# Attention in rounds of four steps in place of two, with one exponential instruction for both heads

## What is computed

```
x = x + _L0_attn_a_ref(_layernorm(x), ...)   # state space: scan over tokens, gelu, norm
x = x + _L0_ffn_ref(_layernorm(x), ...)      # channel mixer with token shift
x = x + _L0_attn_b_ref(_layernorm(x), ...)   # causal attention, 16 heads of 64
x = x + _L0_ffn_ref(_layernorm(x), ...)      # the same mixer again
```

```
latent_kv = x @ w_kv_down                     # 256 -> 128
kv = latent_kv @ w_kv_up; k, v = ...          # 16 heads of 64 each
q = (x @ w_q).reshape(Bx, Tx, N_HEAD, HEAD_SIZE)
att = jnp.einsum('bqhd,bkhd->bhqk', q, k) * scale
att = jnp.where(causal, att, -jnp.inf)
att = jax.nn.softmax(att, axis=-1)
y = jnp.einsum('bhqk,bkhd->bqhd', att, v).reshape(Bx, Tx, HD)
return y @ w_out
```

## Time and profile before

| | |
|---|---|
| median of 3 runs | 2115.67 us (2113.73 to 2116.21) |
| profiled execution, first to last instruction | 2113.7 us |
| its own time | not given apart from the span |
| mean granted TensorE clock | 0.980 |
| TensorE busy | 1984.7 us, 94% |
| VectorE busy | 1337.2 us, 63% |
| ACT busy | 1097.9 us, 52% |
| GpSimd busy | 1425.9 us, 67% |

### The profile page before, as it was taken

The page is one execution under the profiler, slowest core; times in us unless marked ns, Lnnn a source line. Parts: engine busy times, 40 slices in busy tenths (PEclk is TensorE's granted clock), DMA queues, the critical chain, the costliest instruction groups (busy, mean ns, idle before and its releaser), DMA issues.

```text
span 2113.7 us, 35206 instructions
## 1 busy us (share of the span) xinstructions
PE 1984.7 (94%) x12886; PEld 1240.9 (59%) x12886; DVE 1337.2 (63%) x2728; ACT 1097.9 (52%) x2236; POOL 1425.9 (67%) x812
## 2 busy tenths in 40 slices
PE   8997788999999999999989999999999999999898
PEld 6775454555655555555555655555555555555466
DVE  7786555576656666666665657576756575656443
ACT  5775543455545454545455444545445445444585
POOL 1333225778687878787857687868786878687822
PEclk9998899999999999999999999999999999999999
DMA  3000000000000000000000000000000000000001
GB/s 124 1 1 1 0 7 13 13 19 10 13 18 16 13 19 12 19 10 19 13 12 17 12 20 11 17 12 20 11 18 11 20 11 18 11 14 11 26 26 60
DMA packets 29243, 37.01 MB, mean 18 GB/s; under 512 B 6928, under 2 KB 20368, under 8 KB 29072
## 3 DMA queue, kind: packets, MB, share of 16 engines
q1 hardware_dynamic: 29072, 34.76, 5.4%
HBM read 30.02 MB, written 4.46 MB: 16 GB/s over the span
## 4 chain that ended last, share of the span: by engine, by line
PE 63%; DVE 14%; POOL 12%; ACT 6%; issue 4%; DMA 1%; POOLq 0%; ACTq 0%; SPq 0%; DVEq 0%
PE heads_out L918 16%; POOL acc L1416 10%; PE beside L723 9%; PE scores L723 7%; PE two_heads L874 7%; PE scores L897 4%; PE scores L903 4%; PE scores L899 4%; PE scores L901 4%; DVE part_max L1112 3%; ACT prob L1331 2%; PE two_heads L723 2%; PE beside L929 2%; PE heads_out L723 1%; DVE wQK_lo L1073 1%
## 5 line engine op out<-in xcount | busy, mean ns | idle before, releaser
L1416 POOL TENSOR_TENSOR acc<-acc,prob 128x1024 f32<-128x1024 f32 (+3 forms) x512 | 1017.9, 1988 | 195.4 <-ACT prob L1331 140.1
L1331 ACT ACTIVATE prob<-scores 128x512 f32<-128x512 f32 (+3 forms) x1280 | 579.4, 539 | 649.2 <-PE scores L903 289.0
L1112 DVE TENSOR_REDUCE part_max<-two_heads 128x2 f32<-128x1024 f32 x384 | 469.3, 1222 | 280.5 <-PE two_heads L874 279.7
L918 PE MATMUL heads_out<-prob,V 128*64 128x512 f32 (+3 forms) x2560 | 544.4, 547 | 0.0
L1109 DVE CUSTOM_DVE_ANT_0 two_heads<-two_heads,mask 128x128 f32<-128x128 f32 (+3 forms) x512 | 242.0, 514 | 180.4 <-PE two_heads L874 180.4
L874 PE MATMUL two_heads<-k_hi,q_hi 64*128 64x512 f32 (+3 forms) x1280 | 274.1, 424 | 62.8 <-DVE part_max L1112 30.6
L918 PEld LDWEIGHTS heads_out<-prob,V 128*64 128x64 f32 x2560 | 156.7, 137 | 232.4 <-issue 209.6
L874 PEld LDWEIGHTS two_heads<-k_hi,q_hi 64*128 64x128 f32 x1280 | 120.6, 184 | 256.6 <-issue 133.4
L897 PE MATMUL scores<-q_hi,k_hi 64*128 64x512 f32 (+3 forms) x1280 | 236.1, 364 | 0.8 <-DVE k_lo L1100 0.5
L903 PE MATMUL scores<-neg_max,sel 64*128 64x512 f32 (+3 forms) x1280 | 235.6, 362 | 0.0
L901 PE MATMUL scores<-q_lo,k_hi 64*128 64x512 f32 (+3 forms) x1280 | 235.5, 362 | 0.0
(11 more groups left out here) (301 smaller groups left out, 2898.7 us busy)
## 6 DMA issues: line engine op xcount, KB each, us to landing
rden<-rden_rows SPq DMA_DIRECT2D x128, 128.0 KB, 2.9
X<-u SPq DMA_DIRECT2D x8, 512.0 KB, 8.7
out<-X SPq DMA_DIRECT2D x8, 512.0 KB, 2.9
wQK_raw<-wQuery SPq DMA_DIRECT2D x16, 192.0 KB, 3.1
wO_raw<-wOut SPq DMA_DIRECT2D x16, 128.0 KB, 2.8
wV_raw<-wValue SPq DMA_DIRECT2D x8, 128.0 KB, 2.9
den<-den_rows SPq DMA_DIRECT2D x64, 4.0 KB
rden_rows<-den SPq DMA_DIRECT2D x64, 4.0 KB, 1.3
```

The source lines that it names most:

```text
L918: made = pe.matmul(heads_out[head(h), x0:], V[vn % NVS][:, tt, p % 2, head(h)], prob[step % NPROB][:, h, x0:], start=t == 0, stop=t == TPB ...
L1112: made = ve.reduce_max(part_max[:, t, :, c:c + 1], two_heads[:, :, 0:width], AX.X)
L1331: ac.activation(prob[step % NPROB][:, h, x0:], bank(task, h)[:, x0:], ACT.Exp).then_inc(empty(task, h)[0], 1)
L1416: po.tensor_tensor(total[:, :, x0:], total[:, :, x0:], new[:, :, x0:], ALU.add).then_inc(acc_ok, 1)
```

## The change

A round has four steps. Its order is: a maximum, two score tasks, a maximum, the due `invert`, two more score tasks, the rest of the maxima (the first of them in banks 5 and 6, the next in banks 0 and 1, a third in banks 2 and 3), then the four `weigh` and `accumulate` of the same round with `two_parts` after the second of them, `scale_out`, then up to four side tasks in banks 7, 3, 2 and 1 (`SIDE`); `denominators` takes the place of the first, and the fourth runs only if it is due within 8 steps. The products with V are no longer one round behind. `maximum` takes the pair of banks that the plan names (`pair_of`). A score task has both its banks as one entry, with one semaphore step for both heads, and ACT's exponential is one instruction over both heads. Due times at a unit's end and those of the last mixer's first tasks move by some steps.

```diff
 NG = 3
+SIDE = [7, 3, 2, 1]
 DVE_OUT = 62
...
-        self.side_bank = 7
+        self.side_bank, self.max_bank = 7, 5
...
         elif kind == "maximum":
-            self.take(task, (5, 6))
+            self.take(task, (self.max_bank, self.max_bank + 1))
         elif kind == "score":
             n = 2 * (self.step_of[task[1:]] % 2)
             if task[2] >= TPB * UNITS[task[1]][2]:
                 self.masked[task[1:]] = len(self.masked) + 1
-            self.take(task, (n,), (n + 1,))
+            self.take(task, (n, n + 1))
...
-        ahead = {-14: [("channel_start", "b"), ("mixer_weights", "b"), ("turn_normal", "b", 0)],
-                 -12: [("turn", "b", 0), ("turn_normal", "b", 1)], -10: [("turn", "b", 1), ("mix_tokens", "b", 0)],
-                 -4: [("turn_normal", "b", 2)], 0: [("mix_tokens", "b", 1)]}
+        ahead = {-16: [("channel_start", "b"), ("mixer_weights", "b"), ("turn_normal", "b", 0)],
+                 -12: [("turn", "b", 0), ("turn_normal", "b", 1)], -8: [("turn", "b", 1), ("mix_tokens", "b", 0)],
+                 -4: [("turn_normal", "b", 2), ("mix_tokens", "b", 1)]}
...
-            later.extend([(s + 2, ("denominators", idx)), (s + 6, ("invert", idx)), (s + 8, ("scale_out", idx)), (s + 10, ("two_parts", idx))])
+            later.extend([(s + 4, ("denominators", idx)), (s + 8, ("invert", idx)), (s + 8, ("scale_out", idx)), (s + 12, ("two_parts", idx))])
...
-        for s in range(0, len(steps) + 2, 2):
+        for s in range(0, len(steps), 4):
             self.in_steps = True
-            if s == 2:
-                self.heads_free = self.freed[4]
             for load in sorted(x for x in loads if x[0] <= s and self.layers_done):
                 loads.remove(load)
                 self.need(*load[1])
             for b in [STATS_BEFORE[UNITS[i]] for i in range(NU) if s == self.start[i] and UNITS[i] in STATS_BEFORE]:
                 side += self.mixer_stats(b, 2 if b else 3, NT)
             urgent = max([self.start[i] + TPB * (UNITS[i][2] + 1) for i in range(NU) if self.start[i] <= s + 4])
-            goal = min(len(self.maxima), max(urgent, min(s + 2 + LEAD, self.at + 3))) if self.layers_done else urgent
+            goal = min(len(self.maxima), max(urgent, min(s + 4 + LEAD, self.at + 5))) if self.layers_done else urgent
             if self.at < goal:
                 maximum()
-            due("invert")
             for step in steps[s:s + 2]:
                 self.need("score", *step)
+            if not s:
+                self.in_steps = False
+                yield
+                self.in_steps = True
             if self.at < goal:
                 maximum()
             else:
                 chore()
-            filler(10 ** 6)
-            diagonal = not steps[s:s + 2] or any(t >= TPB * UNITS[idx][2] for idx, t in steps[s:s + 2])
-            if not diagonal:
-                self.side_bank = 0
-                filler(s + 8)
-                self.side_bank = 7
-            while self.at < goal - 1:
+            due("invert")
+            for step in steps[s + 2:s + 4]:
+                self.need("score", *step)
+            self.max_bank = 5
+            while self.at < goal:
                 maximum()
-            for idx, t in steps[max(0, s - 2):s]:
+                self.max_bank = (5, 0, 2)[(5, 0, 2).index(self.max_bank) - 2]
+            self.max_bank = 5
+            if not s:
+                self.heads_free = self.freed[4]
+            for idx, t in steps[s:s + 4]:
                 self.need("weigh", idx, t)
                 self.need("accumulate", idx, t)
+                if (idx, t) == steps[s + 1]:
+                    due("two_parts")
                 if t == TPB * (UNITS[idx][2] + 1) - 1:
                     self.need("take_out", idx)
                     output(idx)
-            if self.at < goal:
-                maximum()
-            due("two_parts")
             due("scale_out")
-            if not due("denominators") and diagonal:
-                filler(s + 8)
+            for n, self.side_bank in enumerate(SIDE):
+                if n or not due("denominators"):
+                    filler(10 ** 6 if n < 3 else s + 8)
+            self.side_bank = 7
             if side:
-                self.add_all(side.pop(0))
+                for piece in (side.pop(0), side.pop(0) if side else []):
+                    self.add_all(piece)
             self.add_all(ahead.get(s - len(steps), []))
             self.in_steps = False
             yield
+        s = len(steps)
...
+        def pair_of(task):
+            first = plan.bank[task][0][0][0]
+            return two_heads if first == 5 else scores[:, first:first + 2, :]
...
-                        made = pe.matmul(two_heads[:, h, 0:width], q[head(h), t * P:(t + 1) * P], k[head(h), 0:width], start=True, stop=True)
+                        made = pe.matmul(pair_of(task)[:, h, 0:width], q[head(h), t * P:(t + 1) * P], k[head(h), 0:width], start=True, stop=True)
...
-                    for h in range(2):
-                        for s, v in free(task, h):
-                            w.wait_ge(s, v)
+                    for s, v in free(task):
+                        w.wait_ge(s, v)
+                    first = plan.bank[task][0][0][0]
                     w.wait_ge(*empty(("query", idx)))
                     w.wait_ge(*empty(("turn_max", idx)))
                     w.wait_ge(*empty(("key", idx - j + c)))
                     w.wait_ge(att_const, 4)
                     for h in range(2):
-                        pe.matmul(bank(task, h)[:, x0:], k_hi[g][head(h), kc], q_hi[i][head(h), x0:], start=True, stop=False)
+                        pe.matmul(scores[:, first + h, x0:], k_hi[g][head(h), kc], q_hi[i][head(h), x0:], start=True, stop=False)
                     for h in range(2):
-                        pe.matmul(bank(task, h)[:, x0:], k_lo[g][head(h), kc], q_hi[i][head(h), x0:], start=False, stop=False)
+                        pe.matmul(scores[:, first + h, x0:], k_lo[g][head(h), kc], q_hi[i][head(h), x0:], start=False, stop=False)
                     for h in range(2):
-                        pe.matmul(bank(task, h)[:, x0:], k_hi[g][head(h), kc], q_lo[i][head(h), x0:], start=False, stop=False)
+                        pe.matmul(scores[:, first + h, x0:], k_hi[g][head(h), kc], q_lo[i][head(h), x0:], start=False, stop=False)
                     for h in range(2):
-                        pe.matmul(bank(task, h)[:, x0:], sel[head(h), :], neg_max[idx % NMAX][head(h), x0:], start=False, stop=True).then_inc(full(task, h)[0], 1)
+                        made = pe.matmul(scores[:, first + h, x0:], sel[head(h), :], neg_max[idx % NMAX][head(h), x0:], start=False, stop=True)
+                    made.then_inc(full(task)[0], 1)
                 elif kind == "weigh":
                     _, idx, t = task
                     j = UNITS[idx][2]
                     c, tt = divmod(t, TPB)
                     x0, step = tt * P if c == j else 0, step_of[idx, t]
-                    for h in range(2):
-                        w.wait_ge(*empty(("score", idx, t), h))
+                    w.wait_ge(*empty(("score", idx, t)))
...
                     else:
-                        made = ve.reduce_max(part_max[:, t, :, c:c + 1], two_heads[:, :, 0:width], AX.X)
+                        made = ve.reduce_max(part_max[:, t, :, c:c + 1], pair_of(task)[:, :, 0:width], AX.X)
...
-                        for h in range(2):
-                            w.wait_ge(*full(task, h))
+                        w.wait_ge(*full(task))
                         ve.tensor_tensor(scores[:, first:first + 2, x0:x0 + P], scores[:, first:first + 2, x0:x0 + P],
                                          limit[:, :].unsqueeze(1).broadcast_to([P, 2, P]), ALU.min).then_inc(masked, 1)
...
-                        w.wait_ge(*full(("score", *last_step(idx - NQ)), 1))
+                        w.wait_ge(*full(("score", *last_step(idx - NQ))))
...
-                    for h in range(2):
-                        w.wait_ge(*full(task, h))
-                        ac.activation(prob[step % NPROB][:, h, x0:], bank(task, h)[:, x0:], ACT.Exp).then_inc(empty(task, h)[0], 1)
+                    first = plan.bank[task][0][0][0]
+                    w.wait_ge(*full(task))
+                    ac.activation(prob[step % NPROB][:, :, x0:], scores[:, first:first + 2, x0:], ACT.Exp).then_inc(empty(task)[0], 1)
```

More of the change, by code:

```diff
@@ L1108, in vector_program @@
                         for h in range(2):
-                            made = ve.tensor_tensor_reduce(out=two_heads[:, h, 0:width], in0=two_heads[:, h, 0:width], in1=mask[:, BLK - width:], scale=1.0,
+                            made = ve.tensor_tensor_reduce(out=pair_of(task)[:, h, 0:width], in0=pair_of(task)[:, h, 0:width], in1=mask[:, BLK - width:], scale=1.0,
                                                            scalar=MASKED, op0=ALU.add, op1=ALU.max, accum_out=part_max[:, t, h, c:c + 1])
                     else:
```

(4 more changed lines are left out.)

2 lines of the change are left out of this document (1 added, 1 removed).

## The result

| | before | after |
|---|---|---|
| median, same chip | 2114.70 us | 2363.78 us |
| ratio, 95% interval | | 1.1185, 1.1159 to 1.1212 |
| profiled span | 2113.7 us | 2364.8 us |
| mean granted clock | 0.980 | 0.95 |

The change is 11.8% slower. The direction was forecast, the size was not: +249 us in place of +83, and outside the range.

A forecast was written before the change was run, and what follows sets the result against it. TensorE's queue, busy for 94% of the span, was taken as the bound. Terms of -88 - 58 + 53 + 141 + 32 + 3 = +83 us on the 2115.67 us median gave 2199 us, 3.9% slower; range 2080 to 2260.

The forecast's parts named there:

- refills: TensorE at changes of kind of work: 0.55 us saved in each of 160 rounds, 88 us in all.
- gap before a maximum in banks 5, 6, after scores: TensorE's waits for VectorE to reduce the maximum before: nearly all go, 58 us saved, ends 0 and 58.
- waits for exponentials: TensorE waiting on its own round's exponentials: 53 us added over 96 rounds off the diagonal, 141 over 64 diagonal ones.
- side work at the round's end: Remainders after the last side task delay VectorE's reduction of the next maximum: 32 us added, ends 0 and 80.
- transposes: Transposes before the second batch come closer together: some 3 us added.
- rival 5: Gaps in diagonal rounds lower TensorE's clock: 1.6 us lost in each of 64, 2301 us; chance 0.07.
- Rival 4: TensorE's refills stay, belonging to semaphore waits and not to changes of kind: 2287 us; chance 0.03.
- rival 3: Late queries or keys are put in place and TensorE waits 1.5 us, once a unit: 2295 us; chance 0.08.
- Wrong if the clock is under 0.97: A sign against the forecast: TensorE's granted clock falls under 0.97.
- GpSimd as the releaser of exponentials: A sign against the forecast: ACT's exponentials wait for GpSimd; 2.5 us a round if GpSimd's cover were gone.
- Waits of side products for remainders over 60 us: A sign against the forecast: TensorE's side products wait over 60 us for remainders.
- Rival 1: TensorE's new waits are half as long; under 0.91 us a round the change wins: 2085 us; chance 0.20.

The follow-up runs named there:

- warm: The changed kernel with ten unneeded transposes before the third score task and six before the fourth maximum, in diagonal rounds only: 2335.43 us.
- chores_late: The changed kernel with VectorE's weight remainders moved from behind the maxima to behind the products with V: 2311.09 us.
- exp_two: The changed kernel with one exponential and one semaphore step a head in place of the merged ones: 2424.11 us.
- side_early: The changed kernel with the windows of queries and keys opened and due four steps earlier: 2361.34 us.
- cover_loads: cover_clear with the weights of a pair fetched and loaded two rounds earlier: 2194.8 us.
- two_late: exp_one with weight remainders moved behind the products with V, in rounds of two steps: 2152.35 us.
- exp_one: The kernel before, rounds of two kept, with only the merged exponential and one semaphore step for both heads: 2111.1 us.
- cover_clear: chores_late with the reciprocal behind the maxima and, on the diagonal, side tasks before the third score task and the maximum in banks 0 and 1: 2242.73 us.

## Why the prediction was wrong

The sum's terms against what the starts show (a positive number is time lost):

| term | forecast | shown |
|---|---|---|
| refills | -88 | -64 |
| gap before a maximum in banks 5, 6, after scores | -58 | -25 |
| waits for exponentials (gaps after a maximum) | +53 +141 | +199 |
| side work at the round's end | +32 | +34 |
| clock | 0 | +75 |
| gap before the products with V | 0 | +15 |
| other gaps | 0 | -13 |
| not placed (forecast: transposes) | +3 | +25 |

They sum to 246, the attention's own difference.

**The failed step is the clock.** It is the largest single part of what the sum missed, though not all of it: without its 75 us the time would be some 2289 us, still outside the range, and the other misses are named below. I put it at 0, with 0.07 for rival 5, because one gap of 1.22 us before had left it at 1.00, and "the new gaps are divided". The 1.00 of the earlier trace rows is also a mean over 400 us, which holds the drop at 1077 without showing it. Divided gaps don't spare the clock. The two windows shown above are of one kind of round (the same products, the last four steps of a unit, the same side work). TensorE of the one, kernel after:

```profile
681.61 0.39 PE L908 MATMUL scores<-q_hi,k_hi 64*128 64x256 f32 x2 [1.02 <-ACT prob L1341]
...
683.65 0.79 PE L885 MATMUL scores<-k_hi,q_hi 64*128 64x512 f32 x2 [0.39 <-ACT prob L1341]
684.37 3.60 PE L929 MATMUL heads_out<-prob,V 128*64 128x512 f32 x16
...
687.90 0.39 PE L734 MATMUL beside<-wO_hi,oT_hi 128*128 128x256 f32 x1
...
799.72 0.39 PE L908 MATMUL scores<-q_hi,k_hi 64*128 64x256 f32 x2 [0.99 <-ACT prob L1341]
...
801.75 0.49 PE L885 MATMUL scores<-k_hi,q_hi 64*128 64x512 f32 x2 [0.38 <-ACT prob L1341]
802.18 2.38 PE L929 MATMUL heads_out<-prob,V 128*64 128x512 f32 x16
...
804.48 0.39 PE L734 MATMUL beside<-wO_hi,oT_hi 128*128 128x256 f32 x1
```

The window of the drop, kernel after, columns as in the earlier trace rows:

```profile
684.00:686.00 2.00, 2.00 (x6) 0.53 (x6) 1.71 (x2) 0.00 (x0) 1.81 (x2) 0.50 0.00 0
```

The gaps are alike (1.02 and 0.39; 0.99 and 0.38). In the first round the clock was 0.50, the level of 1.2 GHz, between 684 and 686, and its products with V take 3.53 us from start to start; in the second 2.30. From the third score task to the side work it is 6.29 against 4.76 us. Gaps of the same size sometimes bring the clock down and sometimes not, so one gap that didn't is weak evidence; what decides between the two isn't shown. Rival 5 had 1.6 us in each of 64 rounds. TensorE is at the lower level for 181 us of the attention in place of 26, and 161 of the 181 lie in diagonal rounds; at half speed the difference is at most 78 us lost, beside the 75 of the table. The Trainium skill, TensorE: Matmul & The Clock Gate, "A second HAM failure mode: psum-queue depth-cycling", warns of small idle times between groups that cycle through PSUM banks. I had set it aside because the kernel before cycles through banks as well. The traces agree on the small idle times: the kernel before has 187 gaps over 0.15 us in its attention, the one after 538, and warm, which fills some of them, gets clock back. Whether the cycling through banks has a part in it, no run here shows.

**The second step is an omission.** Weight remainders on VectorE were in no term. They stand where `chore()` puts them, which is now between the scores and the masks of the same round: 53 us in all (chores_late), of which 22 are gaps inside the +199 and 24 are clock inside the +75. I had moved `chore()` with its round and costed only what TensorE and ACT do in it.

**Refills** gave 64 for 88. The change of kind of work does cost about what I read in the earlier trace rows, but a wait in front of a change takes its refill with it, and there are more waits now; the refills behind them are counted as gaps. That is my reading of the 24 us; no run tried it apart. Rival 4 fell, since small excesses did fall by 40%.

**Maxima's waits.** I took the end, 58, of a term from 0 to 58. The gaps after scores fell by 25 and the view's waits by 35: where two maxima follow each other, or a query comes late, the first still waits.

**Waits for exponentials.** Both steps forecast away from the diagonal, the exponential's start and the third score task, are right to 0.05 us in the round shown. The +199 holds 18.5 us for a key's remainder and 22 by weight remainders, so what the exponentials themselves cause is about 158, below the 194 forecast. The merged exponential was taken as 1.05; it comes every 0.98. That it "shows only in the waits above" was right as far as it goes: in exp_two the longer waits bring lower clock as well, and the two together make the 60 us.

**Side work** at +34 met the forecast of +32, by queries mostly; rival 3 in its own form, late due times, fell with side_early.

**What was to be seen.** The order halves the changes of kind, as forecast. Waits for exponentials over 150 us: the view has 131, the starts 158. A diagonal round took over 1 us more than two of before: yes, 2.7. The others "about as long": no, 0.8 us longer, of which some 0.3 may be side work that stood in diagonal rounds before. "Wrong if the clock is under 0.97": it was 0.95, so the prediction named its own failure. GpSimd as the releaser of exponentials: hardly, for 6.4 us in 4 places, where before it had 74.5 in 36. Waits of side products for remainders over 60 us: not seen.

Rival 1, that new waits would be half as long, asked for under 0.91 us a round. They were 199 / 160 = 1.24 by the starts, and the clock put 0.47 on top. Even cover_loads loses.

What stays open: the 25 us not placed, the share of the mask in the diagonal's waits, which wasn't tried apart, and the rounds away from the diagonal, where most of cover_loads' loss lies.

## What to carry to other kernels

A longer round saves refills only if no engine has to finish something of the same round while TensorE stands in front of it. Before widening a round, list for each matmul that reuses a bank or a buffer what has been queued on VectorE and ACT since, weight preparation included: a small job that is free in one order was worth 53 us in another, and moving it cost 41 us in the order of before (two_late against exp_one).

Price new gaps on TensorE twice, as idle time and as clock: here 211 us of gaps brought 75 us of lower clock. With the weight remainders out of the way, useful matmuls in the gaps gave 68 us where idle ones gave 14.

The same edit can be worth nothing or 60 us. Ask first whether TensorE waits for that engine.

## What the runs showed of the hardware

**A VectorE subtraction with two SBUF inputs stands still beside a GpSimd instruction.** The remainder `wQK_lo` of 256 columns takes 0.42 us at 830.74 in the kernel after, while GpSimd does nothing:

```profile
830.74 0.42 DVE L1084 TENSOR_TENSOR wQK_lo<-wQK_raw,wQK_hi 128x256 fp32r<-128x256 f32 x1
...
831.10 0.43 DVE L1132 TENSOR_TENSOR scores<-scores,limit 128x256 f32<-128x256 f32 x1
```

At 833.27, with half the columns, it takes 2.04 us. GpSimd's addition had begun at 832.80 and takes 2.36, so it ended at 835.16 and the remainder at 835.31. In the kernel after, 31 weight remainders of the attention start while a GpSimd instruction runs: the 15 of 128 columns end 0.15 us after it and the 16 of 256 columns 0.28 after it. The rule has exceptions elsewhere: in cover_clear one at 456.51 takes 0.35 us inside a GpSimd addition of 512 columns that began 0.40 us ahead of it. That addition takes 1.87 us, where those of its size took 1.29 on average before, so there GpSimd may have been the one that waited. VectorE's masks and maxima, which read PSUM, keep their times beside GpSimd: 0.72 for two masks and 1.20 for a maximum in the same stretch. The Trainium skill, GPSIMD Engine Reference, "1. Specifications", says that GpSimd's SBUF interfaces are shared with VectorE and that instructions with two SBUF inputs contend. The trace agrees; what I hadn't expected is that a job of 0.4 us can take as long as GpSimd's, 2.4 us (2.41 at 715.08), and stop the queue of masks behind it. A query's remainder, one input from PSUM, stays at 0.69.

**A short drop of the clock cost 1.5 us** here: 6.29 against 4.76 us above. The whole rounds, 11.45 against 9.56, differ by 0.36 more, which are longer gaps ahead of the drop. The drop of the earlier trace rows cost 1.6.
